# The first row bias of a fused cross-attention kernel formed by TensorE, with x loaded later and the second batch's turned x ahead of the late weights

## The reference, cut to what matters

```python
# block 0: softmax over the 512 queries, then residual and layer norm
q = x @ Wq0 + bq0;  k = ctx @ Wk0 + bk0;  v = ctx @ Wv0 + bv0
w = softmax(q @ k.T / 16, axis=queries)
y = layernorm(w @ v + x) * gamma + beta
# block 1: softmax over the 1601 keys, output projection, residual
Q = y @ Wq1 + bq1;  K = ctx @ Wk1 + bk1;  V = ctx @ Wv1 + bv1
out = y + softmax(Q @ K.T / 16, axis=keys) @ V @ Wo + bo
```

```
s = ctx . (A0 x^T + Wk0 bq0)  +  (x Wq0 bk0 + bq0.bk0),     A0 = Wk0 Wq0^T
```

## Time and profile before

| | |
|---|---|
| median of 3 runs | 459.2 us (459.0 to 460.92) |
| profiled execution | 460.37 us, of which the span 458.4 |
| PE busy | 430.9 us, 94% |
| DVE busy | 369.7 us, 81% |
| ACT busy | 366.1 us, 80% |
| POOL busy | 312.6 us, 68% |
| granted TensorE clock, mean | 0.989 of full |

### The profile page before, as it was taken

How to read it: one execution, slowest core, us unless ns; L and a number is a source line. 1 busy time by engine, 2 the same in 40 slices (tenths; PEclk the granted TensorE clock), 3 DMA queues, 4 the chain that set the end, 5 groups by cost and what they waited for, 6 DMA issues and landing times.

```text
span 458.4 us, 7304 instructions
## 1 busy us (share of the span) xinstructions
PE 430.9 (94%) x2192; PEld 340.9 (74%) x2192; DVE 369.7 (81%) x871; ACT 366.1 (80%) x776; POOL 312.6 (68%) x279
## 2 busy tenths in 40 slices
PE   7799799999999999999999999999999989897796
PEld 5555577788778877787788877787778876586696
DVE  3678887789778998799878998799788887586775
ACT  3877499989799878989799878988988788853473
POOL 1586489937996599847995599846995589813400
PEclk9999799999999999999999999999999999998999
DMA  8943012112132032302131032302200010000001
GB/s 273 287 140 93 19 54 72 48 46 74 48 98 65 1 117 73 94 0 76 45 115 48 1 117 74 93 1 68 54 1 1 0 46 2 1 1 23 24 1 46
DMA packets 31190, 28.00 MB, mean 61 GB/s; under 512 B 2856, under 2 KB 26032, under 8 KB 31152
## 3 DMA queue, kind: packets, MB, share of 16 engines
q1 hardware_dynamic: 30736, 27.41, 19.7%
q10 hardware_dynamic: 416, 0.14, 0.1%
HBM read 23.35 MB, written 4.19 MB: 60 GB/s over the span
## 4 chain that ended last, share of the span: by engine, by line
PE 73%; DVE 12%; ACT 6%; issue 3%; SPq 3%; DMA 2%; POOL 1%; DVEq 0%; ACTq 0%; POOLq 0%
PE ps_s L643 11%; PE ps_s L645 9%; PE ps_s L644 9%; PE ps_s L765 9%; PE ps_l L643 7%; PE ps_l L705 7%; PE ps_l L645 7%; PE ps_l L644 7%; ACT p L976 2%; DVE max L1170 2%; PE ps_l L669 2%; DMA xT_sb<-in_xT_dram 2%; DVE xhT_lo L1153 2%; DVE s_sb L1086 1%; DVE y_res L1213 1%
## 5 line engine op out<-in xcount | busy, mean ns | idle before, releaser
L1287 POOL TENSOR_TENSOR wsum<-wsum,p 128x512 f32<-128x512 f32 (+1 forms) x88 | 115.1, 1308 | 15.2 <-ACT p L925 7.5
L1294 POOL TENSOR_TENSOR p_lo<-p,p_hi 128x512 fp32r<-128x512 f32 (+1 forms) x49 | 63.8, 1303 | 44.9 <-ACT p_hi L933 44.7
L919 ACT ACTIVATE p<-s_sb,min 128x512 f32<-128x512 f32 (+1 forms) x104 | 75.0, 721 | 16.0 <-PE ps_l L705 9.5
L925 ACT ACTIVATE p<-p,r 128x512 f32<-128x512 f32 (+1 forms) x104 | 73.0, 720 | 7.0 <-DVE r L1093 6.9
L1086 DVE CUSTOM_DVE_ANT_0 s_sb<-ps_l,cb 128x512 f32<-128x512 f32 (+1 forms) x104 | 70.1, 686 | 10.2 <-PE ps_l L645 6.1
L1170 DVE TENSOR_REDUCE max<-ps_s 128x1 f32<-128x804 f32 x58 | 57.5, 993 | 16.4 <-PE ps_s L645 14.9
L1098 DVE TENSOR_TENSOR p1T_lo<-ps_s,p1T_hi 128x512 fp32r<-128x512 f32 (+1 forms) x91 | 59.8, 684 | 11.6 <-ACT p1T_hi L984 10.9
L984 ACT CAST p1T_hi<-ps_s 128x512 fp32r<-128x512 f32 (+1 forms) x91 | 51.2, 586 | 17.3 <-PE ps_s L765 9.8
L976 ACT ACTIVATE p<-ps_s,bias 128x1206 f32<-128x1206 f32 (+1 forms) x58 | 53.1, 920 | 3.8 <-DVE bias L1181 3.7
L705 PE MATMUL ps_l<-p,ctx_sb 128*128 128x512 f32 (+1 forms) x110 | 55.4, 596 | 0.0
L643 PE MATMUL ps_l<-qw_hi,ctxT_lo 128*128 128x512 f32 (+1 forms) x104 | 51.3, 493 | 1.2 <-DVE ctxT_lo L1047 0.8
(11 more groups left out here) (161 smaller groups left out, 1039.7 us busy)
## 6 DMA issues: line engine op xcount, KB each, us to landing
ctxT_sb<-in_ctxT_dram SPq DMA_DIRECT2D x24, 256.0 KB, 2.7
ctx_sb<-in_ctx_dram SPq DMA_DIRECT2D x24, 256.0 KB, 3.2
xT_sb<-in_xT_dram SPq DMA_DIRECT2D x8, 512.0 KB, 3.8
x_sb<-in_x_dram SPq DMA_DIRECT2D x8, 512.0 KB, 4.1
out_dram<-y_res SPq DMA_DIRECT2D x16, 256.0 KB, 2.2
p<-in_wqT_dram SPq DMA_DIRECT2D x2, 256.0 KB, 4.0
ctxT_sb<-in_ctxT_dram SPq DMA_DIRECT2D x8, 32.5 KB, 1.8
ctx_sb<-in_ctx_dram SPq DMA_DIRECT2D x8, 32.5 KB
```

The lines of the kernel that those rows point to most:

```text
L919: nc.scalar.activation(p0[0:m, ring0(i), :], s0_sb[0:m, (a + i) % 2, :], ACT.Exp, bias=min0[0:m, i:i + 1], scale=-1.0, accum_out=sum0[0:m, ...
L925: nc.scalar.activation(p0[0:m, ring0(i), :], p0[0:m, ring0(i), :], ACT.Copy, scale=r0[0:m, i:i + 1]).then_inc(norm0_done, 1)
L1287: nc.gpsimd.tensor_tensor(total, total, p0[0:m, ring0(i), :], ALU.add).then_inc(wsum_done, 1)
L1294: nc.gpsimd.tensor_tensor(p0_lo[0:m, h, :], p0[0:m, ring0(i), :], p0_hi[0:m, h, :].bitcast(F32), ALU.subtract).then_inc(p0_lo_done, 1)
```

## The change

The row bias of batch 0 is formed by TensorE alone. `make_w0` step 2 makes u0 also as a column, in two halves of 128 (four products of one column each), and copies it out with the other small columns. A new step `project_bias0_first` multiplies that column, broadcast to 128 columns, with turned x of batch 0: the product is the row bias on all partitions. It goes into bank 1 of `ps_s1` (`cb_bank`), not into `ps_misc`. VectorE's multiply and sum for batch 0 are gone. `make_w0` step 1 (u0 as a row, still wanted by GpSimd for batch 1) moves behind the first score tile, and its copy on ScalarE behind `bias0`. SP loads x of batch 0 only after the second weights, turned x, ctxT and ctx of batch 1. Turned x of batch 1 waits for `project_q0` and for the new step of batch 0.

```diff
 TENSOR_HEAD = (
-    ("make_w0", 0, 0), ("make_w0", 0, 1), ("make_w0", 0, 2), ("project_q0", 0, 0), ("project_bias0", 0, 0),
-    ("scores0", 0, 0), ("scores0", 0, 1), ("make_w1", 0, 0), ...
+    ("make_w0", 0, 0), ("make_w0", 0, 2), ("project_q0", 0, 0), ("project_bias0_first", 0, 0), ("scores0", 0, 0),
+    ("make_w0", 0, 1), ("scores0", 0, 1), ("make_w1", 0, 0), ...
...
             def load_xT(c):
 
                 if c >= 1:
                     sp.wait_ge(qw0_ps, c)
+                    if c == 1:
+                        sp.wait_ge(cb_ps, c)
...
             def pre0():
                 sp.dma_start(wqT[0], wqT0.rearrange("(h p) e -> p h e", p=P)).then_inc(w_loaded[0], 16)
                 load_xT(0)
-                load_ctxT(0, 0)
-                load_x(0)
-                load_ctx(0, 0)
-                for g in range(1, GROUPS):
+                for g in range(GROUPS):
                     load_ctxT(0, g)
                     load_ctx(0, g)
                 sp.dma_start(wqT[1], wqT1.rearrange("(h p) e -> p h e", p=P)).then_inc(w_loaded[1], 16)
                 sp.dma_start(wkT[1], wkT1.rearrange("(h p) l -> p h l", p=P)).then_inc(w_loaded[1], 16)
+                load_xT(1)
+                load_ctxT(1, 0)
+                load_ctx(1, 0)
+                load_x(0)
                 sp.dma_start(wv0_sb, wv0).then_inc(wv_loaded, 16)
...
+            def project_bias0_first(a, _):
+
+                pe.wait_ge(small_sb[0], 1)
+                for c in range(EC):
+                    mm = nc.tensor.matmul(cb_bank(0), u0_col[:, c:c + 1].broadcast_to([P, P]), xT_sb[:, c, :],
+                                          start=(c == 0), stop=(c == EC - 1))
+                mm.then_inc(cb_ps, 1)
...
+                    for c in range(EC):
+                        for h in range(EC):
+                            mm = nc.tensor.matmul(ps_acc0[:, 2 + c:3 + c], wqT[0][:, h, c * P:(c + 1) * P], bk_col[0][:, h:h + 1],
+                                                  start=(h == 0), stop=(h == EC - 1))
...
-            def weigh_u0_first(a, _):
-
-                dve.wait_ge(u0_done, 1)
-                dve.wait_ge(x_loaded[0], 16)
-                nc.vector.tensor_tensor(xr[:], x_sb[0][:], u0_row[:].unsqueeze(1).broadcast_to([P, TB, E]), ALU.mult
-                                        ).then_inc(xu0_done, 1)
...
             def weigh_u0(a, _):
...
                 if a == 1:
-                    pool.wait_ge(z0_done, a)
+                    pool.wait_ge(u0_done, 1)
```

42 lines of the change are left out of this document (24 added, 18 removed), and 48 rows, old and new, of tables (TENSOR_HEAD, VECTOR_HEAD).

## The result

The changed kernel took 465.57 us in the median of 4 runs (462.68 to 466.32), the kernel before 459.78 beside it (4 runs, 459.0 to 460.92): a ratio of 1.0131, 95% interval 1.0097 to 1.0166. It is 1.3% slower. The forecast was 463.1 with a range up to 464.6: the side was right, the size was not, and the time lies 1 us outside the range. The profiled execution of the changed kernel is its fastest one, 462.68 us with a span of 460.7; the other three, which have no profile, had spans of 464.4, 464.2 and 463.1. That gap of 2.4 to 3.7 us between executions of one program has to be explained too.

The account below looks back on a forecast made before the run. Bound: chain of waits through turned x (1.98 us TensorE idle) and batch 1's z, then a steady block where TensorE hardly pauses. Head 0, stall gain not kept, z +0.9, clock +3.0: +3.9 on 459.2 gives 463.1; range 458.2 to 464.6.

Parts of the forecast that it names:

- The head, called even: Up to the first exponentials: 0.5 us gained, then 0.4 lost, taken as 0, with ends of -0.5 and +0.6.
- Turned x issued near 11.7, the stall of 1.98 gone but not kept: SP issues batch 1's turned x after the bias product; TensorE's 1.98 us idle goes, but TensorE then waits for z.
- x(1)'s landing: Batch 1's x, last in SP's load order, was to land at 25.5 us, with ends of 24.6 and 26.5.
- GpSimd, the ring and tile 6: GpSimd's product waits for x(1), delaying the sums that free exponentials' ring places; tile 6 at 29.2 instead of 26.50.
- an estimate of 20.9 for x(1): Landing by the skill's rule, 2.0 us fixed plus bytes over 436 GB/s: as early as before, GpSimd not late.
- all of it now waits for the bias product: On SP, turned x and the loads behind it wait for TensorE's bias product; nothing issued for some microseconds until 11.7.
- the clock, 3.0 us: After TensorE's idle before z, about 6.0 us of work at half pace, 3.0 lost; with z's 0.9, TensorE 3.9 late.
- ScalarE's 2.0: ScalarE enters its gapless stretch of exponentials 2.0 us late, behind tile 7; TensorE's 3.9 more than covers it.
- 0.9 of z: Batch 1's sum z on VectorE, behind tile 6's reciprocal, ends at 31.4 against 30.51: 0.9 us late.
- Case B: Rival: GpSimd late but TensorE's clock stays full, ScalarE's +2.0 decides: 461.2 us; chance 0.25.
- Case C: Rival: x(1) lands early, so the kernel gets faster: 457.7 us, or 457.2 with the stall's gain kept whole; chance 0.15.
- z, no longer behind VectorE's sum of two weight rows, 2 us early as well: Part of Case C: with x(1) landing at 21.5, batch 1's z comes 2 us early and the stall's 1.98 is kept.

Follow-up runs that it names:

- e10: The changed kernel's first bias on TensorE, with the loads in the order of the kernel before; ratio 1.0019 to the kernel before.
- e3: The changed kernel with GpSimd's product of x(1) and u0 moved behind the sums of tiles 2 to 4; 460.64 us, ratio 1.0042 to the kernel before.
- e8: The changed kernel with step 1 of VectorE's weight preparation moved right behind step 0; 463.32 us, ratio 1.0079 to the kernel before.
- e1: The changed kernel run and profiled once more, no edit; 464.97 us (5 runs), ratio 1.0130 to the kernel before.
- e4: The changed kernel with eighteen identity products filling TensorE's idle time ahead of batch 1's z; 465.18 us, ratio 1.0142 to the kernel before.
- e2: The changed kernel with x(1) loaded ahead of x(0) and the late weights; 458.72 us (12 runs), ratio 0.9993 to the kernel before.
- e9: The kernel before with only x(1) issued late, behind the second batch's third group; 465.15 us, ratio 1.0134 to the kernel before.
- e6: The kernel before with TensorE's first weight product made to wait until turned ctx has landed; ratio 1.0003 to the kernel before.
- e7: The changed kernel with TensorE's first weight product made to wait until turned ctx has landed; 467.8 us, ratio 1.0188 to the kernel before.
- e15: The changed kernel with x(1), late weights and broadcast rows issued before batch 1's turned x, x(0) later; 456.17 us, ratio 0.9939 to the kernel before.

## Why the prediction was wrong

**The head, called even.** Right. TensorE's first score tile came at 11.48 (forecast 11.6 to 11.7), tile 0's exponential at 14.11 for 14.06, and e10 leaves 1.0019, an interval that holds 1.

**Turned x issued near 11.7, the stall of 1.98 gone but not kept.** Right in the profiled execution: 11.64, and no idle ahead of 20.10. It is 11.65 in e3, but 12.05 in e8, 12.78 in e1 and 13.08 in e4, with nothing changed ahead of it, which is the first failed step, below.

**x(1)'s landing.** The forecast was 25.5, its far end 26.5; measured 26.22. From the issue of turned x it was 14.6 us where the forecast had 13.8, and 15.1 in e1.

**GpSimd, the ring and tile 6.** Right: 2.37 and 1.23 us behind the landing, tile 6 at 29.92 (forecast 29.2, late by the 0.7 of x(1)), tile 7 at 31.33 (30.6), z ended at 32.05 (31.4), so that TensorE started on it 1.55 us late, not 0.9, after an idle of 4.61 us (5.1). e2, e3 and e9 show that this chain makes the loss; e10 shows that the rest of the change adds nothing that its interval can tell (at most 0.4%). The forecast weighed this against the Trainium skill, DMA: Bandwidth & Descriptors, section Anatomy of one DMA, and had an estimate of 20.9 for x(1) from it; measured is 5.3 us later. That is no test of the rule: the section states it for one transfer that GpSimd issues, and the forecast used it for twelve in a row that SP issues.

**The first failed step: "all of it now waits for the bias product".** It stands in the forecast with one fixed time beside it, 11.7, and the sum has no term for a later one. It was not asked how firm that time is, nor what the kernel before did with a TensorE that starts late. One profile shows one start. The warm-up products take 3.87 us in one execution and 4.63 in another, and with the products behind them TensorE reaches the bias product 1.1 us later. In the kernel before this is lost in the 1.98 us that TensorE waits for turned x anyway (e6: 1.7 us later, ratio 1.0003). In the changed kernel turned x, the weights, the rows and x(1) all go through it (e7). The profiled execution has +3.88 at the mark, as forecast; e1, of the common kind, has +5.87. Added to 459.2, the first gives 463.1 and the second 465.1, and the range ended at 464.6: by these two profiles it is this 2 us that puts the median outside (of the result's other three executions there are only the times). And the stall that was removed was also the cover of the start.

**The second failed step: the clock, 3.0 us.** The fall to half clock was forecast and came, but lasted 3.1 us of work, not 6.0, and e4 shows 0.2 to 0.5 us for it. The work at half clock lies beside ScalarE, which is busy without a gap from 29.92 to 39.27 and is as late. The forecast took the larger of the two delays, TensorE's 3.9 and ScalarE's 2.0; ScalarE's was the one that counted. (e3, where ScalarE is on time at tile 8, shows that the same half clock is not free everywhere.)

**What stood in its place.** ScalarE's 2.0 was also too small: tile 8 is 2.57 us late, tile 9 2.58. Then VectorE's weight step collides with GpSimd's belated sums; ScalarE waits 1.73 for it, and tiles 11 and 12 are 4.4 us late, batch 1's first tile on VectorE 3.79. e8 prices this at 2.0. The lateness of the profiled execution adds up so: 3.4 us at tile 6, 2.6 at tile 8, plus 1.9 by the collision is 4.4 at tile 11, less 0.6 that is taken up again by the mark is 3.9. The forecast had 0.9 of z and 3.0 of the clock, which is 3.9 as well. It was right to 0.1 us for this one execution, and by luck. Case B, in which the clock stays and the time is 461.2, had no place for a collision and would have been wrong too.

**Case C.** Its mechanism, given 0.15, is sound, only not in this order of loads: with x(1), weights and rows early and z's path free, e15 measured 0.9939 of before (0.9921 to 0.9957) where C's 457.2 is 0.9956. Its "z, no longer behind VectorE's sum of two weight rows, 2 us early as well" came as 1.69 us at TensorE (28.86 for 30.55), and z is still behind that sum, which has become short.

What stays open: why the warm-up takes 3.87 us or 4.63. Both starts are at 1.56 and both clock columns read full there, though TensorE gets through half as many products in a microsecond at first: 6 from 3 to 4 us in both, then 11 from 5 to 6 in the result's profile where e1 has 7, and e1 has 13 only from 7 to 8.

## What to carry to other kernels

When a load that waits for an engine is moved ahead of loads that wait for nothing, all of these inherit that engine's jitter (its varying start); look for what absorbed it before, which is often the very stall that is being removed. Put what needs no wait ahead of it: e15 issues x(1), the weights and the rows in the time in which SP stood idle, and that turns 1.3% lost into 0.6% won. And a small operation on VectorE is to be priced by what GpSimd does beside it in the new timing, not by its duration in the old one.
